# A two-layer graph network on one core: ScalarE's row-by-row tile gathers go to GpSimd, and twenty small gathers are added near the start

## The chip, the cores and the metric

The kernel runs on one core of a Trainium2 chip. The metric is device time in microseconds (us). Engines are named as the profile names them: PE is TensorE (PEld its weight loads), DVE is VectorE, ACT is ScalarE, POOL is GpSimd, SP is SyncE, which here only issues transfers. A q behind a name (ACTq, SPq) marks the work of the engine's instruction queue, such as issuing a transfer.

## The reference, cut to what matters

`x` has 12500 nodes of 256 float32 features; 200000 edges run from `src` to `dst`, sorted by `dst`.

```python
# layer 0
scale = sqrt(out_deg[src]) * sqrt(out_deg[dst])
msg   = (t1[src] + (feat[src] * feat[dst]) @ W2) / scale[:, None]     # t1 = feat @ W1
agg   = segment_sum(msg, dst)
embed = leaky_relu(where(in_cnt > 0, t1 + agg, 0) + b0)
x     = layernorm(x + embed / max(norm(embed), 1e-12))
# layer 1
xt    = x @ W.T + b1
out   = segment_sum(xt[src], dst) / (deg + 1)
x     = layernorm(x + out)
```

Both layers are linear in the gathered rows up to the sum, so the kernel gathers and sums rows of a table first (`x` scaled by the root of the degree in layer 0, the first layer's output in layer 1) and multiplies by the weights afterwards, once for each node and not for each edge.

## The kernel before

The edges are cut into tiles of 128. A **round** is 32 tiles (`U`), in four quarters or groups of 8 (`QT`, `GT`); there are 49 rounds in each of the two layers, and the last has 27 tiles. While a round's edges are summed, the two blocks of 128 nodes that the round before completed are finished (weights, activation, normalization).

**Gather.** Tile u of a round needs the 128 table rows that its edges name, 1 KB each, in slot u of `ring`, an SBUF buffer of 32 slots. For most tiles GpSimd issues one indirect transfer (`gather_quarter`, line 470): one instruction fetches all 128 rows by a column of `idx`. For tile 31 (`HAND_U`) of rounds 2 to 47 this is done otherwise, row by row. In even rounds SyncE does it (`gather_by_hand`): it loads 16 row numbers at a time into registers (line 360) and issues one transfer of one row for each (lines 362 and 363), 128 in all, into a side buffer; `hand_to_ring` (line 370) copies that into the slot once the round before is done with it. In odd rounds ScalarE does the same (`gather_by_act`, lines 631 to 635; `act_hand_to_ring`, line 641), in pieces of 24, 16 and 24 rows (`ACT_ROWS`) in each of two rounds. Both side buffers lie in space that an earlier stage has left (`src_lo`, `src_hi`). A pair of rounds has thus 62 gathers by GpSimd, 128 row transfers by SyncE and 128 by ScalarE; there are 23 pairs (`HAND_PAIRS`) in each layer.

**Sum.** VectorE builds one-hot matrices from `dst` (line 821), TensorE multiplies them with the gathered rows (line 1120), a group of 8 tiles adding up in one PSUM bank, and signals `groups_done`. VectorE adds the group to the two node blocks it can touch (line 847).

**Refill.** When a group is done, ScalarE copies the next 8 index columns for the same quarter of the next round (`refill`, line 579), which lets GpSimd gather that quarter. ScalarE's program is a fixed order: refill 0, 24 rows, refill 1, its share of finishing the last node blocks (lines 586 to 601), refill 2, two square roots that wait for VectorE (607, 609), 16 rows, refill 3, 24 rows. An instruction that waits holds up all behind it on its engine.

SyncE's order in a pair is: load and store the node blocks of one round (`next_pair`), copy its tile into the ring, wait for it, 64 rows, `next_pair` again, 64 rows, load the next 128 indices.

**Start.** GpSimd first gathers 32 tiles of raw `x` and 32 columns of the factors `r` (line 478), then waits until the scaled table is stored and a flag is made, and enters its loops. The flag chooses between this path and a slow one for unordered edges, which does not run here.

Of the kernel before, what the change touches and what calls it, by code (L numbers as in the profile page):

```python
# [24 lines left out]
P = 128  # L25
D = 256
KF = D // P
NODES = 12500
# [5 lines left out]
U = 32  # L34
# [35 lines left out]
DUMP = NPAD  # L70
HAND_U = U - 1
HAND_REGS = 16
ACT_ROWS = {0: (0, 24), 2: (24, 40), 3: (40, 64)}
HAND_PAIRS = (ROUNDS - 2) // 2


def gnn(nc, x, src, dst, w1, w2, b0, wl, b1, out):
# [6 lines left out]
    with ExitStack() as ctx:  # L84
# [19 lines left out]
        src_hi = sb("src_hi", [P, TILES], BF16)  # L104
        hands = [src_lo[:, 2 * n * D:2 * (n + 1) * D].bitcast(F32) for n in range(2)]
        hand_idxs = [src_hi[0:1, 2 * n * P:2 * (n + 1) * P].bitcast(I32) for n in range(2)]
        count_to = sb("count_to", [P, P, PAIR], BF16)
# [115 lines left out]
        gather_turn = sem("gather_turn")  # L223
        hand_idx_in = [sem(f"hand_idx_in{n}") for n in range(2)]
        hand_rows_in = [sem(f"hand_rows_in{n}") for n in range(2)]
        sync_turn = sem("sync_turn")
        hand_in_ring = [sem(f"hand_in_ring{n}") for n in range(2)]
        dst_hot_made = sem("dst_hot_made")
# [42 lines left out]
        def _(sp):  # L271
# [76 lines left out]
            def load_hand_idx(layer, j):  # L348

                sp.dma_start(hand_idxs[0][:, :],  # L350
                             src[bass.ds((2 * j + 2) * U * P + HAND_U * P, P)].rearrange("(a n) -> a n", a=1)
                             ).then_inc(hand_idx_in[0], 16)

            def gather_by_hand(layer, j, half):

                if half == 0:
                    sp.wait_ge(hand_idx_in[0], 16 * (hand_no(layer, j) + 1))
                    sp.sem_inc(sync_turn, 1)
                for first in range(half * P // 2, (half + 1) * P // 2, HAND_REGS):
                    sp.load(hand_regs, hand_idxs[0][0:1, first:first + HAND_REGS])  # L360
                    for k in range(HAND_REGS):
                        row = sp.snap(hand_regs[k], min_val=0, max_val=NODES - 1)  # L362
                        sp.dma_start(hands[0][first + k:first + k + 1, :],  # L363
                                     table[layer][bass.ds(row, 1), :]).then_inc(hand_rows_in[0], 16)

            def hand_to_ring(layer, j):

                sp.wait_ge(hand_rows_in[0], 16 * P * (hand_no(layer, j) + 1))
                sp.wait_ge(groups_done, group_no(layer, 2 * j + 1, GR - 1) + 1)
                sp.dma_start(ring[:, HAND_U, 0:D], hands[0][:, :]).then_inc(hand_in_ring[0], 16)  # L370

            def hand_pair(layer, j):

                next_pair(layer, 2 * j)
                hand_to_ring(layer, j)
                sp.wait_ge(hand_in_ring[0], 16 * (hand_no(layer, j) + 1))
# [7 lines left out]
            with sp.If(disordered == 0):  # L384
                for c in range(len(X_CHUNKS)):
                    sp.wait_ge(table_stored[c], 16)
                for layer in range(2):
# [9 lines left out]
                    hand_to_ring(layer, HAND_PAIRS - 2)  # L397
                    sp.wait_ge(hand_in_ring[0], 16 * (hand_no(layer, HAND_PAIRS - 2) + 1))
                    gather_by_hand(layer, HAND_PAIRS - 1, 0)
# [34 lines left out]
        def _(g):  # L434
# [52 lines left out]
            for u in range(RAW):  # L487
                gather_r(u)
            for c in range(len(X_CHUNKS)):
                g.wait_ge(table_stored[c], 16)  # L490
            g.wait_ge(flag_made, 1)
            disordered = g.value_load(flag[0:1, 0:1], min_val=0, max_val=1)
            with g.If(disordered == 0):
                for layer in range(2):
                    if layer == 1:
                        g.wait_ge(table1_whole, 1)
                    for i in range(0 if layer == 1 else 1, 2):
                        for q in range(4):
                            gather_quarter(layer, i, q)
                    with g.Fori(2, ROUNDS - 1) as i:  # L500
                        for q in range(4):
                            gather_quarter(layer, i, q, HAND_U)
                    for q in range(4):
                        gather_quarter(layer, ROUNDS - 1, q, FINAL)
# [25 lines left out]
        def _(act):  # L530
# [79 lines left out]

            act_regs = [act.alloc_register(f"act_row{k}") for k in range(24)]

            def act_hand_no(layer, j):

                return layer * HAND_PAIRS + j

            def load_act_idx(layer, j):

                nc.scalar.dma_start(hand_idxs[1][:, :],
                                    src[bass.ds((2 * j + 3) * U * P + HAND_U * P, P)].rearrange("(a n) -> a n", a=1)  # L620
                                    ).then_inc(hand_idx_in[1], 16)

            def gather_by_act(layer, j, half, q):

                if half == 0 and q == 0:
                    act.wait_ge(hand_idx_in[1], 16 * (act_hand_no(layer, j) + 1))
                    act.sem_inc(act_turn, 1)
                    act.wait_ge(hand_in_ring[1], 16 * (act_hand_no(layer, j) + 1))
                    act.sem_inc(act_turn, 1)
                first, end = (half * P // 2 + n for n in ACT_ROWS[q])  # L630
                act.load(act_regs[0:end - first], hand_idxs[1][0:1, first:end])  # L631
                for k in range(first, end):
                    row = act.snap(act_regs[k - first], min_val=0, max_val=NODES - 1)  # L633
                    nc.scalar.dma_start(hands[1][k:k + 1, :],  # L634
                                        table[layer][bass.ds(row, 1), :]).then_inc(hand_rows_in[1], 16)

            def act_hand_to_ring(layer, j):

                act.wait_ge(hand_rows_in[1], 16 * P * (act_hand_no(layer, j) + 1))
                act.sem_inc(act_turn, 1)  # L640
                nc.scalar.dma_start(ring[:, HAND_U, 0:D], hands[1][:, :]).then_inc(hand_in_ring[1], 16)

            def round_(layer, i, finish, pair_no=None, half=0):
                if pair_no is not None and half == 0:
                    load_act_idx(layer, pair_no)
                for q in range(4):
                    if finish and q == LAST_K + 1:
                        if layer == 0:
                            clear_sums(i - 1)
                        else:  # L650
                            act.wait_ge(groups_added, group_no(layer, i, LAST_K + 1) + SUMS)
                            take_sums(i - 1, acc[:, bass.ds(2 * i - 2, 2), :])
                        take_turned(layer, i - 1)
                    refill(layer, i, q)
                    if finish and q == LAST_K + 1:
                        roots(layer, i - 1)
                    if pair_no is not None and q in ACT_ROWS:
                        gather_by_act(layer, pair_no, half, q)
                if pair_no is not None and half == 1:
                    act_hand_to_ring(layer, pair_no)  # L660

            act.wait_ge(flag_made, 1)
            disordered = act.value_load(flag[0:1, 0:1], min_val=0, max_val=1)
            with act.If(disordered == 0):
                act.sem_inc(hand_in_ring[1], 16)
# [344 lines left out]
        def _(pe):  # L1010
# [94 lines left out]

            def round_(layer, i, finish, end=U, by_hand=None, pair_no=0):

                for k in range(GR):
# [26 lines left out]
            with pe.If(disordered == 0):  # L1135
                for layer in range(2):
                    round_(layer, 0, False)
                    round_(layer, 1, True)
                    with pe.Fori(0, HAND_PAIRS) as j:
                        round_(layer, 2 * j + 2, True, by_hand=0, pair_no=j)  # L1140
                        round_(layer, 2 * j + 3, True, by_hand=1, pair_no=j)
                    round_(layer, ROUNDS - 1, True, FINAL)
# [41 lines left out]
```

## Time and profile before

| | |
|---|---|
| timed, median of 2 runs | 4644.35 us (4642.15 to 4646.56) |
| profiled execution, from its first to its last instruction | 6311.9 us, 85381 instructions |
| PE busy | 2685.6 us (43%), 9623 matmuls |
| DVE busy | 1596.4 us (25%) |
| ACT busy | 448.2 us (7%) |
| POOL busy | 2936.4 us (47%), 3087 instructions |
| mean granted TensorE clock | 0.672 of full speed |
| DMA | 506.28 MB, 80 GB/s on average |

The profile comes from an execution of its own. The only time known of it is its span, and that is 1668 us more than the timed median: where very many small instructions are recorded, the recording takes time itself. Issuing of transfers, register work and waits are not counted as busy, so an engine can be fully occupied and still show a small share, as ScalarE and SyncE do here. The profile's chain of waits follows the work that ended last back to what released it; "issue" is time in which an engine waited for nothing that the profile shows.

### The profile page before, as it was taken

Reading aid. Unit: us, or ns where it says so; the run is one execution under the profiler, and the core shown is the slowest. Engines: PE = TensorE matmul, PEld = TensorE weight load, DVE = VectorE, ACT = ScalarE, POOL = GpSimd, SP = SyncE. Lnnn points to the kernel's source line nnn. Section 1 sums busy time; section 2 is a strip of 40 time slices with the busy share of each in tenths; the row PEclk is TensorE's granted clock in tenths of the full one; section 3 lists DMA queues with packets and bytes.
Section 4 is the critical chain, followed back from the end, with each engine's and each line's share of the span. In section 5 each row is a group of like instructions: output and inputs, shape, how many; then the busy total and the mean of one; then the engine's idle time right before and its main releaser. Section 6 shows DMA issues by size and latency. Waiting matters only on the chain.

```text
span 6311.9 us, 85381 instructions
## 1 busy us (share of the span) xinstructions
PE 2685.6 (43%) x9623; PEld 1864.3 (30%) x9623; DVE 1596.4 (25%) x3315; ACT 448.2 (7%) x1457; POOL 2936.4 (47%) x3087
## 2 busy tenths in 40 slices
PE   6344444444444444434454343434343434343434
PEld 5233333332333333323232222222232322222223
DVE  9522222222222222222231111212121212121212
ACT  9300000000000000000000000000000000000000
POOL 3444444444444444444445444444444444444444
PEclk8676666666666666666666666666666666666667
DMA  4322222222222222222222222222222222222222
GB/s 125 118 76 78 78 74 80 77 80 76 80 77 78 76 79 79 77 78 79 77 79 82 74 81 75 80 76 79 75 83 77 79 77 81 77 78 79 77 80 79
DMA packets 270181, 506.28 MB, mean 80 GB/s; under 512 B 69534, under 2 KB 172557, under 8 KB 269645
## 3 DMA queue, kind: packets, MB, share of 16 engines
q0 software_dynamic: 146656, 397.89, 22.1%
q1 hardware_dynamic: 104496, 91.77, 4.7%
q10 hardware_dynamic: 18492, 12.11, 0.7%
q14 instruction: 522, 4.27, 0.2%
q8 instruction: 15, 0.25, 0.0%
HBM read 450.89 MB, written 38.54 MB: 78 GB/s over the span
## 4 chain that ended last, share of the span: by engine, by line
SPq 45%; issue 40%; ACTq 7%; DVE 3%; PE 3%; DMA 1%; DVEq 1%; another core or an unknown queue 1%; ACT 0%
SPq L363 27%; SPq L362 9%; SPq L360 5%; ACTq L634 4%; DVE hot_space L711 2%; PE banks L1120 1%; ACTq L633 1%; ACTq L631 1%; PE banks L1099 1%; SPq L323 1%; SPq L319 1%; SPq L310 1%; DMA ring<-src_lo 1%; DVEq L703 1%
## 5 line engine op out<-in xcount | busy, mean ns | idle before, releaser
L1120 PE MATMUL banks<-ring,hot_space 128*128 128x257 f32 x6252 | 2080.3, 479 | 989.9 <-issue 931.7
L470 POOL DMA_INDIRECT ring<-x,idx x1517 | 1435.6, 946 | 1616.6 <-ACT idx L579 1130.9
L470 POOL DMA_INDIRECT ring<-scaled_x,idx x1485 | 1410.1, 950 | 1595.7 <-ACT idx L579 1161.7
L1120 PEld LDWEIGHTS banks<-ring,hot_space 128*128 128x128 f32 x6252 | 1362.8, 236 | 1657.6 <-issue 1414.6
L847 DVE SCALAR_TENSOR_TENSOR big<-banks,here_mask,big 128x257 f32 x784 | 343.1, 479 | 2835.2 <-PE banks L1120 1309.0
L1088 PE MATMUL banks<-ident,halves 128*128 128x128 f32 x588 | 140.2, 396 | 1584.3 <-ACT halves L592 1294.1
L1099 PE MATMUL banks<-w_s,a_t 128*128 128x256 f32 x784 | 285.0, 542 | 943.0 <-ACT a_t L601 943.0
L1088 PEld LDWEIGHTS banks<-ident,halves 128*128 128x128 f32 x588 | 97.2, 199 | 1630.3 <-ACT halves L592 1313.8
L821 DVE TENSOR_TENSOR hot_space<-banks,dst_rel 128x1024 f32<-128x1024 f32 x395 | 483.7, 1225 | 183.1 <-issue 182.6
L1099 PEld LDWEIGHTS banks<-w_s,a_t 128*128 128x128 f32 x784 | 218.4, 286 | 1013.3 <-ACT a_t L601 966.0
L579 ACT COPY idx<-src_col 128x8 int32 (+1 forms) x392 | 77.6, 198 | 4897.8 <-issue 4286.1
L871 DVE SCALAR_TENSOR_TENSOR e<-banks,scal,b_s 128x256 f32<-128x256 f32 x98 | 42.9, 479 | 1162.9 <-PE banks L1099 625.2
L547 ACT ACTIVATE dst_rel<-columns,halves 128x128 bf16<-128x128 f32 x576 | 161.3, 374 | 4.5 <-DVE halves L740 4.5
L857 DVE SCALAR_TENSOR_TENSOR halves<-x_t,root,big 128x256 f32<-128x256 f32 x98 | 47.4, 483 | 277.6 <-DMA x_t<-in_x 255.5
L1027 PE MATMUL banks<-hot_space 128*128 128x98 bf16 x1280 | 90.2, 235 | 41.3 <-DVE hot_space L711 40.5
L1099 PE MATMUL banks<-wt_s,a_t 128*128 128x256 f32 x392 | 107.0, 422 | 0.1
L711 DVE TENSOR_TENSOR hot_space<-src_lo,count_to 128x2048 bf16<-128x2048 bf16 x80 | 97.6, 1220 | 0.2
L1099 PEld LDWEIGHTS banks<-wt_s,a_t 128*128 128x128 f32 x392 | 89.2, 228 | 18.6 <-ACT a_t L601 0.5
L1027 PEld LDWEIGHTS banks<-hot_space 128*128 128x128 bf16 x1280 | 76.8, 113 | 52.9 <-DVE hot_space L711 45.9
L601 ACT COPY a_t<-banks 128x512 f32<-128x512 f32 (+1 forms) x196 | 87.8, 478 | 45.6 <-PE banks L1088 44.6
L478 POOL DMA_INDIRECT r_edge<-r_table,idx x32 | 31.5, 985 | 112.1 <-DMA r_table<-e 102.7
L711 DVE TENSOR_TENSOR hot_space<-src_hi,count_to 128x1568 bf16<-128x1568 bf16 x80 | 77.5, 969 | 0.0
(112 smaller groups left out, 798.8 us busy)
## 6 DMA issues: line engine op xcount, KB each, us to landing
src_lo<-scaled_x SPq DMA_DIRECT2D x2944, 1.0 KB
src_lo<-scaled_x ACTq DMA_DIRECT2D x2944, 1.0 KB
src_lo<-x SPq DMA_DIRECT2D x2944, 1.0 KB
src_lo<-x ACTq DMA_DIRECT2D x2944, 1.0 KB
ring<-x,idx POOLq DMA_INDIRECT x1517
ring<-scaled_x,idx POOLq DMA_INDIRECT x1485
x<-out_t SPq DMA_DIRECT2D x98, 128.0 KB
x_t<-x SPq DMA_DIRECT2D x98, 128.0 KB
```

The source lines that it names most:

```text
L360: sp.load(hand_regs, hand_idxs[0][0:1, first:first + HAND_REGS])
L362: row = sp.snap(hand_regs[k], min_val=0, max_val=NODES - 1)
L363: sp.dma_start(hands[0][first + k:first + k + 1, :], table[layer][bass.ds(row, 1), :]).then_inc(hand_rows_in[0], 16)
L470: g.indirect_dma_start(ring[:, u, 0:D], None, table[layer], bass.IndirectOffsetOnAxis(ap=idx[:, u:u + 1], axis=0)).then_inc(rows_in[u], 16)
L634: nc.scalar.dma_start(hands[1][k:k + 1, :], table[layer][bass.ds(row, 1), :]).then_inc(hand_rows_in[1], 16)
L711: last = nc.vector.tensor_tensor(hots[half], vals.unsqueeze(2).to_broadcast(shape), count_to[:, 0:size, :].unsqueeze(1).to_broadcast(shape ...
L821: last = nc.vector.tensor_tensor(dst_hot[:, buf, :, :], lane_row.unsqueeze(1).to_broadcast([P, GT, P]), rel, ALU.is_equal)
L847: last = nc.vector.scalar_tensor_tensor(here, group_sum(k), here_mask[:, n, bass.ds(i * GR + k, 1)], here, ALU.mult, ALU.add)
L1027: last = nc.tensor.matmul(hist, lo_hot[half][:, t // PAIR, :, t % PAIR], hi_hot[half][:, t // PAIR, :, t % PAIR], start=first and t == 0, ...
L1088: last = nc.tensor.transpose(turned[s][:, place:place + P], halves[:, s, h, k * P:(k + 1) * P], ident[:, :])
L1099: last = nc.tensor.matmul(project[s], left, right, start=n == 0, stop=n == len(parts) - 1)
L1120: last = nc.tensor.matmul(group_sum(k), dst_hot[:, k % HOTS, u - k * GT, :], ring[:, u, 0:DW], start=u == tiles[0], stop=u == tiles[-1])
```

## The change

ScalarE's gathers are removed whole: its registers, index loads, row transfers, the copy into the ring, and `ACT_ROWS`; its loop is one plain loop over rounds 1 to 48. GpSimd gathers all 32 tiles in odd rounds and 31 in even ones; its loop body holds two rounds. TensorE waits for tile 31 of an odd round on `rows_in[31]`. SyncE's part is the same with new names. New are twenty gathers from `x` by GpSimd (`LOOKS`), in five turns of four, of 128 down to 8 rows, into four slots of unused space in `src_lo` and `src_hi`; after each turn GpSimd waits until all four have landed. They stand between the gathers of `r` and the wait for the table, and nothing reads what they bring.

```diff
+LOOKS = ((P, P, P, P), (64, 64, 32, 32), (127, 127, 126, 125), (124, 120, 112, 96), (16, 16, 8, 8))
-ACT_ROWS = {0: (0, 24), 2: (24, 40), 3: (40, 64)}
...
+        looks = [part[:, 2 * n * D:2 * (n + 1) * D].bitcast(F32) for part in (src_lo, src_hi) for n in (1, 2)]
...
             for u in range(RAW):
                 gather_r(u)
+            def early_look(no, rows, slot):
+                g.indirect_dma_start(looks[slot][0:rows, :], None, x,
+                                     bass.IndirectOffsetOnAxis(ap=src_col[0:rows, no:no + 1], axis=0)
+                                     ).then_inc(looks_in[slot], 16)
+            taken = [0] * len(looks)
+            for turn, sizes in enumerate(LOOKS):
+                for slot, rows in enumerate(sizes):
+                    early_look(turn, rows, slot)
+                    taken[slot] += 16
+                for slot in range(len(sizes)):
+                    g.wait_ge(looks_in[slot], taken[slot])
+                    g.sem_inc(gather_turn, 1)
...
-                    with g.Fori(2, ROUNDS - 1) as i:
+                    with g.Fori(0, HAND_PAIRS) as j:
                         for q in range(4):
-                            gather_quarter(layer, i, q, HAND_U)
+                            gather_quarter(layer, 2 * j + 2, q, HAND_U)
+                        for q in range(4):
+                            gather_quarter(layer, 2 * j + 3, q)
...
-            def gather_by_act(layer, j, half, q):
-                if half == 0 and q == 0:
-                    act.wait_ge(hand_idx_in[1], 16 * (act_hand_no(layer, j) + 1))
-                    act.sem_inc(act_turn, 1)
-                    act.wait_ge(hand_in_ring[1], 16 * (act_hand_no(layer, j) + 1))
-                    act.sem_inc(act_turn, 1)
-                first, end = (half * P // 2 + n for n in ACT_ROWS[q])
-                act.load(act_regs[0:end - first], hand_idxs[1][0:1, first:end])
-                for k in range(first, end):
-                    row = act.snap(act_regs[k - first], min_val=0, max_val=NODES - 1)
-                    nc.scalar.dma_start(hands[1][k:k + 1, :],
-                                        table[layer][bass.ds(row, 1), :]).then_inc(hand_rows_in[1], 16)
...
                     refill(layer, i, q)
                     if finish and q == LAST_K + 1:
                         roots(layer, i - 1)
-                    if pair_no is not None and q in ACT_ROWS:
-                        gather_by_act(layer, pair_no, half, q)
-                if pair_no is not None and half == 1:
-                    act_hand_to_ring(layer, pair_no)
...
-                    with act.Fori(0, HAND_PAIRS) as j:
-                        round_(layer, 2 * j + 1, True, j, 0)
-                        round_(layer, 2 * j + 2, True, j, 1)
-                    round_(layer, ROUNDS - 2, True)
-                    round_(layer, ROUNDS - 1, True)
+                    with act.Fori(1, ROUNDS) as i:
+                        round_(layer, i, True)
...
-                        if u == HAND_U and by_hand is not None:
-                            pe.wait_ge(hand_in_ring[by_hand], 16 * (layer * HAND_PAIRS + pair_no + 1 + by_hand))
+                        if u == HAND_U and by_hand:
+                            pe.wait_ge(hand_in_ring, 16 * (layer * HAND_PAIRS + pair_no + 1))
                         elif u == HAND_U:
-                            pe.wait_ge(rows_in[u], 16 * (layer * 2 + i + 1))
+                            rounds_before = layer * (HAND_PAIRS + 2) + (i if pair_no is None else pair_no + 2)
+                            pe.wait_ge(rows_in[u], 16 * (rounds_before + 1))
```

## Rows read from the trace of the kernel before

**Rows 1.** The page: span, and the chain that ended last by engine.
```profile
span 6311.9 us, 85381 instructions
...
SPq 45%; issue 40%; ACTq 7%; DVE 3%; PE 3%; DMA 1%; DVEq 1%; another core or an unknown queue 1%; ACT 0%
```

**Rows 2.** Line 470, GpSimd's gathers: ns min/median/max; then idle us, times, until whom.
```profile
L470 POOL DMA_INDIRECT ring<-x,idx x1517: 940/946/1207, 3277.1 to 6284.9; - x190
L470 POOL DMA_INDIRECT ring<-scaled_x,idx x1485: 940/946/1195, 254.3 to 3232.7; - x186
...
  ACT idx L579: 2292.5, 288
```

**Rows 3.** Timeline of GpSimd: start us, us, instruction, [idle before, us, <- its releaser].
```profile
227.00 0.94 POOL L478 DMA_INDIRECT r_edge<-r_table,idx  x1 [0.30 <-issue]
254.33 0.94 POOL L470 DMA_INDIRECT ring<-scaled_x,idx  x1 [26.39 <-ACT idx L579]
...
297.97 0.95 POOL L470 DMA_INDIRECT ring<-scaled_x,idx  x1 [0.30 <-issue]
...
3200.23 0.94 POOL L470 DMA_INDIRECT ring<-scaled_x,idx  x1 [9.61 <-ACT idx L579]
...
3277.11 0.94 POOL L470 DMA_INDIRECT ring<-x,idx  x1 [43.44 <-SPq L337]
...
3369.54 0.94 POOL L470 DMA_INDIRECT ring<-x,idx  x1 [4.16 <-ACT idx L579]
...
6247.58 0.94 POOL L470 DMA_INDIRECT ring<-x,idx  x1 [9.08 <-ACT idx L579]
```

**Rows 4.** Waits over the whole span: who, for what: us, times, longest.
```profile
ACT idx L579 <- issue: 4286.1, 273, 24.3
```

**Rows 5.** Timeline of ScalarE in one steady pair of rounds, 1505 to 1649 us.
```profile
1508.18 13.01 ACTq L634 DMA_DIRECT2D src_lo<-scaled_x  x24
1521.46 0.20 ACT L579 COPY idx<-src_col 128x8 int32 x1 [14.94 <-issue]
...
1535.67 13.02 ACTq L634 DMA_DIRECT2D src_lo<-scaled_x  x16
...
1550.82 15.08 ACTq L634 DMA_DIRECT2D src_lo<-scaled_x  x24
...
1574.12 13.12 ACTq L634 DMA_DIRECT2D src_lo<-scaled_x  x24
...
1602.01 12.79 ACTq L634 DMA_DIRECT2D src_lo<-scaled_x  x16
...
1616.92 14.46 ACTq L634 DMA_DIRECT2D src_lo<-scaled_x  x24
...
1633.54 14.11 ACTq L634 DMA_DIRECT2D src_lo<-scaled_x  x24
```

**Rows 6.** Timeline of SyncE's row transfers in four stretches.
```profile
231.96 22.03 SPq L363 DMA_DIRECT2D src_lo<-scaled_x  x46
...
256.27 37.96 SPq L363 DMA_DIRECT2D src_lo<-scaled_x  x24
...
1502.65 58.08 SPq L363 DMA_DIRECT2D src_lo<-scaled_x  x64
...
1564.65 50.97 SPq L363 DMA_DIRECT2D src_lo<-scaled_x  x64
...
1628.88 9.86 SPq L363 DMA_DIRECT2D src_lo<-scaled_x  x18
...
3280.11 65.11 SPq L363 DMA_DIRECT2D src_lo<-x  x24
```

**Rows 7.** Timeline of ScalarE, 3143 to 3154 us, in which SyncE issues nothing.
```profile
3143.10 10.49 ACTq L634 DMA_DIRECT2D src_lo<-scaled_x  x24
```

**Rows 8.** Timeline of TensorE at the start of the second layer.
```profile
3280.01 9.78 PE L1120 MATMUL banks<-ring,hot_space 128*128 128x257 f32 x16 [12.59 <-DMA ring<-x,idx]
...
3312.25 1.20 PE L1120 MATMUL banks<-ring,hot_space 128*128 128x257 f32 x2 [3.00 <-issue]
```

More of the change, by code:

```diff
@@ L104, in gnn @@
         src_hi = sb("src_hi", [P, TILES], BF16)
-        hands = [src_lo[:, 2 * n * D:2 * (n + 1) * D].bitcast(F32) for n in range(2)]
-        hand_idxs = [src_hi[0:1, 2 * n * P:2 * (n + 1) * P].bitcast(I32) for n in range(2)]
+        hand = src_lo[:, 0:2 * D].bitcast(F32)
+        hand_idx = src_hi[0:1, 0:2 * P].bitcast(I32)
+        looks = [part[:, 2 * n * D:2 * (n + 1) * D].bitcast(F32) for part in (src_lo, src_hi) for n in (1, 2)]
         count_to = sb("count_to", [P, P, PAIR], BF16)
@@ L223, in gnn @@
         gather_turn = sem("gather_turn")
-        hand_idx_in = [sem(f"hand_idx_in{n}") for n in range(2)]
-        hand_rows_in = [sem(f"hand_rows_in{n}") for n in range(2)]
+        looks_in = [sem(f"looks_in{n}") for n in range(len(looks))]
+        hand_idx_in = sem("hand_idx_in")
+        hand_rows_in = sem("hand_rows_in")
         sync_turn = sem("sync_turn")
-        hand_in_ring = [sem(f"hand_in_ring{n}") for n in range(2)]
+        hand_in_ring = sem("hand_in_ring")
         dst_hot_made = sem("dst_hot_made")
@@ L348, in load_hand_idx @@
             def load_hand_idx(layer, j):
-                sp.dma_start(hand_idxs[0][:, :],
+                sp.dma_start(hand_idx[:, :],
                              src[bass.ds((2 * j + 2) * U * P + HAND_U * P, P)].rearrange("(a n) -> a n", a=1)
-                             ).then_inc(hand_idx_in[0], 16)
+                             ).then_inc(hand_idx_in, 16)
             def gather_by_hand(layer, j, half):
                 if half == 0:
-                    sp.wait_ge(hand_idx_in[0], 16 * (hand_no(layer, j) + 1))
+                    sp.wait_ge(hand_idx_in, 16 * (hand_no(layer, j) + 1))
                     sp.sem_inc(sync_turn, 1)
                 for first in range(half * P // 2, (half + 1) * P // 2, HAND_REGS):
-                    sp.load(hand_regs, hand_idxs[0][0:1, first:first + HAND_REGS])
+                    sp.load(hand_regs, hand_idx[0:1, first:first + HAND_REGS])
                     for k in range(HAND_REGS):
                         row = sp.snap(hand_regs[k], min_val=0, max_val=NODES - 1)
-                        sp.dma_start(hands[0][first + k:first + k + 1, :],
-                                     table[layer][bass.ds(row, 1), :]).then_inc(hand_rows_in[0], 16)
+                        sp.dma_start(hand[first + k:first + k + 1, :],
+                                     table[layer][bass.ds(row, 1), :]).then_inc(hand_rows_in, 16)
             def hand_to_ring(layer, j):
-                sp.wait_ge(hand_rows_in[0], 16 * P * (hand_no(layer, j) + 1))
+                sp.wait_ge(hand_rows_in, 16 * P * (hand_no(layer, j) + 1))
                 sp.wait_ge(groups_done, group_no(layer, 2 * j + 1, GR - 1) + 1)
-                sp.dma_start(ring[:, HAND_U, 0:D], hands[0][:, :]).then_inc(hand_in_ring[0], 16)
+                sp.dma_start(ring[:, HAND_U, 0:D], hand[:, :]).then_inc(hand_in_ring, 16)
             def hand_pair(layer, j):
@@ L375, in hand_pair @@
                 hand_to_ring(layer, j)
-                sp.wait_ge(hand_in_ring[0], 16 * (hand_no(layer, j) + 1))
+                sp.wait_ge(hand_in_ring, 16 * (hand_no(layer, j) + 1))
                 gather_by_hand(layer, j + 1, 0)
@@ L397, in _ @@
                     hand_to_ring(layer, HAND_PAIRS - 2)
-                    sp.wait_ge(hand_in_ring[0], 16 * (hand_no(layer, HAND_PAIRS - 2) + 1))
+                    sp.wait_ge(hand_in_ring, 16 * (hand_no(layer, HAND_PAIRS - 2) + 1))
                     gather_by_hand(layer, HAND_PAIRS - 1, 0)
@@ L609, in roots, with round_ @@
                 nc.scalar.activation(pair[3], mv[:, :, 1], ACT.Sqrt, bias=epsilon[:, 0:1]).then_inc(var_rooted, 1)
[L611 to L621, printed above, removed]
-            def gather_by_act(layer, j, half, q):
-                if half == 0 and q == 0:
-                    act.wait_ge(hand_idx_in[1], 16 * (act_hand_no(layer, j) + 1))
-                    act.sem_inc(act_turn, 1)
-                    act.wait_ge(hand_in_ring[1], 16 * (act_hand_no(layer, j) + 1))
-                    act.sem_inc(act_turn, 1)
-                first, end = (half * P // 2 + n for n in ACT_ROWS[q])
-                act.load(act_regs[0:end - first], hand_idxs[1][0:1, first:end])
-                for k in range(first, end):
-                    row = act.snap(act_regs[k - first], min_val=0, max_val=NODES - 1)
-                    nc.scalar.dma_start(hands[1][k:k + 1, :],
-                                        table[layer][bass.ds(row, 1), :]).then_inc(hand_rows_in[1], 16)
[L637 to L645, printed above, removed]
+            def round_(layer, i, finish):
                 for q in range(4):
@@ L664, in _ @@
             with act.If(disordered == 0):
-                act.sem_inc(hand_in_ring[1], 16)
                 for c in range(len(X_CHUNKS)):
@@ L1104, in pace, with round_ @@
                 pe.value_load(block_row[0:1, 0:1], min_val=0, max_val=NW - 1)
-            def round_(layer, i, finish, end=U, by_hand=None, pair_no=0):
+            def round_(layer, i, finish, end=U, by_hand=False, pair_no=None):
                 for k in range(GR):
@@ L1139, in _ @@
                     with pe.Fori(0, HAND_PAIRS) as j:
-                        round_(layer, 2 * j + 2, True, by_hand=0, pair_no=j)
-                        round_(layer, 2 * j + 3, True, by_hand=1, pair_no=j)
+                        round_(layer, 2 * j + 2, True, by_hand=True, pair_no=j)
+                        round_(layer, 2 * j + 3, True, pair_no=j)
                     round_(layer, ROUNDS - 1, True, FINAL)
```

## The prediction

> **What bounds the kernel now.** I read the head of the page and the chain first, then the waits of GpSimd and ScalarE, then both engines' instructions in one stretch. All durations come from the one profiled execution, whose span is 6311.9 us; the timed runs have a median of 4644.35 us, 1668 us less [rows 1]. So the recording itself stretches this kernel, most where single instructions are many, and SyncE's share of the chain (45%) is to be read with that in mind. I make the sum against 6311.9 us and then scale only the repeated rounds to the timed median.
>
> GpSimd needs 1.25 us from one gather to the next, whether its queue has just started or has run for many gathers [rows 2, 3]. In the recording it stands still before a gather for 2292.5 us because ScalarE has not yet refilled the indices [rows 2], and ScalarE's refill waits mostly for nothing but its own queue (4286.1 us put down to "issue") [rows 4]. The stretch shows why: after each refill ScalarE issues 24, 16 or 24 row transfers, and the next refill stands right behind the last of them [rows 5]. So in the recording ScalarE sets the pace: refill, rows, refill.
>
> Is this so in the timed runs? The steady rounds 2 to 47 run from 297.97 to 3200.23 us in the first layer and from 3369.54 to 6247.58 us in the second [rows 3]: 5780.3 us for 46 pairs of rounds, 125.7 us each. All the rest is 531.6 us. If that rest costs the same when timed, a timed pair is (4644.4 - 531.6) / 46 = 89.4 us. What can fill 89.4 us? **GpSimd:** 62 gathers x 1.25 = 77.5 us. **SyncE:** 46 rows alone took 22.03 us with their register loads, 0.479 us each [rows 6]; 128 rows are 61.3 us, and between its blocks of 64 rows it spends 3.9 and 13.3 us on loads, stores and the copy into the ring (1560.73 to 1564.65, 1615.62 to 1628.88) [rows 6]: 78.5 us. **ScalarE:** 24 rows alone took 10.49 us, 0.437 each [rows 7], so 128 are 55.9 us; of the pair from 1508.18 to 1633.54 us its six row blocks fill 81.5 us and everything else 43.9 us [rows 5]: 99.8 us. ScalarE is the only one of the three that reaches 89.4 us; part of its 43.9 us (waits for VectorE) must be shorter when timed. I take it as the bound.
>
> **The change part by part.** (1) ScalarE loses, in each of 46 pairs, 128 row transfers with their register work, six register loads, an index load and the copy into the ring. Its queue falls from 99.8 us to at most 43.9 us a pair, below the others, and each refill stands behind the matmuls of its own quarter again. Gain: what the next bound allows. (2) GpSimd gets 46 gathers, 46 x 1.25 = 57.5 us; it will be the bound, so I count them in full: 63 x 1.25 = 78.75 us a pair. The loop body doubles to two rounds, which costs nothing between instructions that follow each other at 0.30 us of issue [rows 3]. (3) TensorE waits for tile 31 of an odd round on that gather's own semaphore instead of the copy into the ring. The gather is GpSimd's last of the round, as late as the copy was or earlier; behind this wait stand the group's end, the VectorE sum and the refill, all of which have three quarters of gathers (some 30 us) as slack: nothing. (4) SyncE keeps its 128 rows a pair, 78.5 us by the floor above. It no longer shares issue time with ScalarE: with ScalarE busy its 64 rows took 58.08 and 50.97 us, 0.91 and 0.80 a row, against 0.479 alone [rows 6].
>
> (5) The twenty early gathers. GpSimd's last gather of r starts at 227.00 us and is over at 228.2 us, and the first table gather waits until 254.33 us [rows 3], for an index refill that hangs on TensorE's first group and not on GpSimd. Twenty gathers at 1.25 us are 25 us. At each of five turns GpSimd waits for the data: from a gather's start at 3277.11 us to the matmul that uses it at 3280.01 us are 2.9 us [rows 3, 8], 1.65 us beyond the pitch, 8.3 us in all. So GpSimd comes to the first table gather at 261.5 us, 7 us late. The trace shows no gather of fewer rows: between a floor of the 0.30 us gap alone (then the idle time hides all, 0 us) and data landing as slowly as beside SyncE's rows (4.2 us from tile to tile [rows 8], 13 us more) the bounds are 0 and 20 us; I take 7, since nearest is the full gather. Behind these waits stand only GpSimd's own gathers.
>
> **The sum.** A pair after: GpSimd 78.75 us, SyncE 78.5 us. Two bounds this close never overlap fully, and gathers slow SyncE's rows: in two stretches with gathers running and ScalarE silent it issued 24 rows in 37.96 and 65.11 us, 1.58 and 2.71 a row [rows 6]. That cannot hold when timed: 128 rows fit into 89.4 - 17.2 = 72.2 us now, 0.564 a row at most. I take 81 us a pair. In the profiled frame: 6311.9 - 5780.3 + 7 = 538.6 us, plus 46 x 81 = 3726: 4265 us. For the likeliest case pairs of 78.75 to 84 us give 4161 and 4403; with 0 for the early gathers 4154. Own range 4150 to 4400.
>
> The row says that issuing a transfer takes ScalarE 0.437 us and that this is what the refills wait for. The Trainium skill (DMA: Bandwidth & Descriptors, "Issuing engines are not separate DMA queues") says that spreading transfers over engines only saves issue time, "usually small relative to the DMA itself"; by it ScalarE's rows would cost next to nothing and their removal would bring nothing, which is the first rival's time.
>
> **The rivals.** *A, GpSimd is already the bound when timed.* Then its gather takes 89.4 / 62 = 1.442 us there, though 1.25 us in the trace, and the change adds 46 x 1.442 = 66 us and some 8 us for the early gathers: 4718 us. For it: the recording's shape is ScalarE's and need not be that of the timed runs. Against it: gathers never slow down with load in the trace (at most 1.207 us busy against a median of 0.946 [rows 2]), and recording adds time, it does not take any away. The Trainium skill (SBUF — State Buffer, "Who interferes with whom") says that GpSimd's generation of descriptors can be shut out while VectorE holds the shared port; that would speak for this rival, and the trace does not agree: 1.207 us is the longest of 3002.
>
> *B, SyncE is the next bound.* The sum holds until its average row passes (78.75 - 17.2) / 128 = 0.481 us. Halfway to today's 0.564, at 0.53, a pair is 85 us: 538.6 + 3910 = 4449 us. For it: 78.5 against 78.75 leaves no room.
>
> *C, slower.* The same queue, starved. Gathers run 77.5 of 89.4 us now and nearly without a break afterwards, and beside them rows are slow [rows 6]. The hand-gathered tile then comes late each second round. It decides from a row of 0.579 us, where a pair reaches 91.3 us and the whole 4737 us; at 0.60 us a pair is 94.0 us and the whole 4863 us. For it: the two slow stretches. Against it: 256 rows and 62 gathers fit into 89.4 us today, the change leaves 128 rows and 63 gathers.
>
> **How the numbers follow.** Forecast 0.55; A 0.20; B 0.15; C 0.10. Predicted 4265 us. The range runs from 4150 (all hidden, GpSimd alone) up to 4720, which takes in B and A's value and leaves out C and the edges. 2% is 93 us (below 4551, above 4737), about what can be told from no change. Faster: forecast and B, 0.70. Same: nearly all of A, and half of what B and C put near the border, 0.20. Slower: C and A's edge, 0.10.
>
> **What would show it.** In the profile after, GpSimd's waits for the refill should fall from 2292.5 us to a few hundred, ScalarE's refill should wait for TensorE's group instead of "issue", GpSimd's pitch should stay 1.25 us, and the first table gather should start near 261 us. SyncE's rows should be nearer 0.48 than 0.9 us where no gathers run. The recorded span should fall less surely than the timed one, because recording stretches SyncE's rows. It would be wrong if GpSimd stood idle as long as before with tile 31 of even rounds late (B, C), or if the timed pair grew by one gather (A).

## The result, and the profile after

The changed kernel takes 4153.61 us (2 runs, 4153.19 to 4154.04) against 4644.35 us: a ratio of 0.893, 95% interval 0.8885 to 0.8979. The forecast was faster and about 4265 us; the gain is 491 us and not 379. Multiplied out, 0.8932 of the median before is 4148 us, just under the low end of the range.

One thing must be said first, since it decides how the recording before is to be read. **The recording of before was made in other surroundings than its timed runs.** A recording does not stretch this kernel: after, the span is 4152.3 us beside timed runs of 4153.6. The kernel before, timed again in five later batches (a batch is a set of kernels timed side by side), took 4640, 6302, 6376, 4641 and 6412 us, and within a batch its runs agreed within 1%. I call these the quick and the slow surroundings. The recording of before (6311.9 us, [rows 1]) was made in the slow surroundings, the 4644.35 us were timed in the quick. What differs between them outside the kernel isn't known: two of the batches, one quick (4640 us) and one slow (6376 us), were reported under the same chip number.

The head and the chain of the page after, and two waits from the trace (who, for what: us, times, longest):

```profile
span 4152.3 us, 67120 instructions
...
POOL 70%; issue 25%; ACT 2%; DMA 1%; PE 1%; POOLq 1%; DVE 1%; DVEq 0%; ACTq 0%; SPq 0%
...
ACT idx L598 <- PE banks L1098: 2511.2, 388, 34.4
...
POOL ring L472 <- issue: 931.6, 3046, 3.5
```

The chain is GpSimd's gathers (line 472 now) with the gap of 0.30 us between them: 70% and 25%. ScalarE's refill (line 598 now) waits for TensorE's group and no longer for its own queue (4286.1 us in [rows 4]). Line 472 by itself, after:

```profile
L472 POOL DMA_INDIRECT ring<-x,idx x1540: 942/946/1215, 2200.1 to 4133.3; - x193
L472 POOL DMA_INDIRECT ring<-scaled_x,idx x1508: 942/946/1226, 275.1 to 2168.8; - x189
its engine sat idle before it (us, times) until:
  issue: 931.6, 3046
  SPq L339: 30.3, 1
  ACT idx L598: 0.3, 1
```

A gather costs what it cost in [rows 2] (median 946 ns), and the wait for the refill has gone to 0.3 us. The 2292.5 us of [rows 2] are from the slow surroundings; the first experiment below, recorded in the quick ones with ScalarE's rows in place, has 641.9 us, and that is the number to compare with:

```profile
POOL ring L473 <- ACT idx L597: 641.9, 224, 9.0
```

GpSimd's timeline after, answering to [rows 3]:

```profile
275.07 0.98 POOL L472 DMA_INDIRECT ring<-scaled_x,idx  x1 [3.48 <-issue]
...
315.33 1.03 POOL L472 DMA_INDIRECT ring<-scaled_x,idx  x1 [0.30 <-issue]
...
2135.95 0.99 POOL L472 DMA_INDIRECT ring<-scaled_x,idx  x1 [0.30 <-issue]
...
2280.06 0.95 POOL L472 DMA_INDIRECT ring<-x,idx  x1 [0.31 <-issue]
...
4100.75 0.95 POOL L472 DMA_INDIRECT ring<-x,idx  x1 [0.30 <-issue]
```

From the second row to the third and from the fourth to the fifth are 23 pairs of rounds each: 1820.6 and 1820.7 us, 79.16 us a pair, of which 63 gathers are 78.75. All the rest is 511.0 us. SyncE's row transfers after:

```profile
1513.51 31.29 SPq L365 DMA_DIRECT2D src_lo<-scaled_x  x64
...
1549.82 31.19 SPq L365 DMA_DIRECT2D src_lo<-scaled_x  x64
```

64 rows in 31.3 us, 0.489 each, beside gathers without a break; the recording of the first experiment, with ScalarE's rows in place, has the same 31.3 us. In [rows 6] rows beside gathers took up to 2.71 us; that was the slow surroundings.

### The profile page after: what moved, and what is told of

It reads as the page before. It is cut to its first block, busy times and chain, and to the rows that moved or that the text cites. A ratio compares the mean times of both kernels' runs of the same rounds, so it can differ in the third digit from the quotient of the medians.

```text
span 4152.3 us, 67120 instructions
## 1 busy us (share of the span) xinstructions
PE 3222.2 (78%) x9623; PEld 1713.0 (41%) x9623; DVE 1603.0 (39%) x3315; ACT 460.6 (11%) x1457; POOL 3015.1 (73%) x3153
## 3 DMA queue, kind: packets, MB, share of 16 engines
q1 hardware_dynamic: 104496, 91.77, 7.0%
## 4 chain that ended last, share of the span: by engine, by line
POOL 70%; issue 25%; ACT 2%; DMA 1%; PE 1%; POOLq 1%; DVE 1%; DVEq 0%; ACTq 0%; SPq 0%
POOL ring L472 68%; ACT dst_rel L566 2%; POOL r_edge L480 1%; DMA src_hi<-in_x,src_col 0%; POOL src_lo L494 0%; PE banks L1076 0%; POOLq L469 0%; DVEq L680 0%; DMA ring<-x,idx 0%; POOLq L470 0%; PE banks L1098 0%; POOLq L517 0%; ACTq L566 0%; DMA ring<-scaled_x,idx 0%; PE banks L1065 0%
## 5 line engine op out<-in xcount | busy, mean ns | idle before, releaser
L1098 PE MATMUL banks<-ring,hot_space 128*128 128x257 f32 x6252 | 2745.4, 551 | 817.3 <-DMA ring<-x,idx 374.5
L1098 PEld LDWEIGHTS banks<-ring,hot_space 128*128 128x128 f32 x6252 | 1281.3, 247 | 2214.3 <-DMA ring<-x,idx 1020.0
L472 POOL DMA_INDIRECT ring<-x,idx x1540 | 1464.9, 951 | 499.5 <-issue 468.9
L472 POOL DMA_INDIRECT ring<-scaled_x,idx x1508 | 1435.5, 952 | 462.7 <-issue 462.7
L1076 PE MATMUL banks<-w_s,a_t 128*128 128x256 f32 x784 | 185.1, 390 | 0.0
L1076 PEld LDWEIGHTS banks<-w_s,a_t 128*128 128x128 f32 x784 | 147.6, 193 | 34.5 <-issue 15.7
L1065 PEld LDWEIGHTS banks<-ident,halves 128*128 128x128 f32 x588 | 115.2, 209 | 45.8 <-issue 21.3
L1076 PEld LDWEIGHTS banks<-wt_s,a_t 128*128 128x128 f32 x392 | 72.2, 194 | 26.6 <-issue 17.9
L903 DVE TENSOR_SCALAR out_t<-out_t,mv,scal 128x256 f32<-128x256 f32 x196 | 75.4, 426 | 7.7
## 6 DMA issues: line engine op xcount, KB each, us to landing
x<-out_t SPq DMA_DIRECT2D x98, 128.0 KB
x_t<-x SPq DMA_DIRECT2D x98, 128.0 KB
x_t<-in_x SPq DMA_DIRECT2D x97, 128.0 KB
```

The source lines that it names most:

```text
L472: g.indirect_dma_start(ring[:, u, 0:D], None, table[layer], bass.IndirectOffsetOnAxis(ap=idx[:, u:u + 1], axis=0)).then_inc(rows_in[u], 16)
L903: nc.vector.tensor_scalar(out_t[s][:, :], out_t[s][:, :], mv[:, s, 0:1], scal[:, 6 + s:7 + s], ALU.subtract, ALU.mult).then_inc(out_ready[ ...
L1065: last = nc.tensor.transpose(turned[s][:, place:place + P], halves[:, s, h, k * P:(k + 1) * P], ident[:, :])
L1076: last = nc.tensor.matmul(project[s], left, right, start=n == 0, stop=n == len(parts) - 1)
L1098: last = nc.tensor.matmul(group_sum(k), dst_hot[:, k % HOTS, u - k * GT, :], ring[:, u, 0:DW], start=u == tiles[0], stop=u == tiles[-1])
```

## The experiments

Two theories stood at first. Q: ScalarE's queue is too long for a pair of rounds, and the early gathers only cost their time. G: the early gathers change how gathers and row transfers share the DMA path, which would explain SyncE's sudden 0.489 us. Times are medians of 4 runs against 7 of the kernel before in the same batch, but for the last experiment.

**Early gathers on the kernel before.** The `LOOKS` block of the change is put into the kernel before, ScalarE's rows stay.

> The kernel before with the twenty early gathers added and ScalarE's row transfers kept. Theory Q (ScalarE's queue is the bound, the early gathers only cost their time at the start): 4644 + 21 = about 4665 us, SyncE's rows beside gathers as slow as before (1.6 to 2.7 us each). Theory G (the early gathers change how later gathers and row transfers share the DMA engines; the profile after has SyncE's rows at 0.50 us beside unbroken gathers): clearly under 4644 us, some 4250 to 4500 us, and SyncE's rows near 0.5 to 0.7 us.

4686.2 us beside 4640.1, ratio 1.0098 (1.0077 to 1.0119): 46 us more, where Q had said 21. G, which wanted a clear gain, is out. This is also a quick recording of ScalarE's part (line 652 issues its rows, 597 is the refill; timeline of one pair of rounds):

```profile
1522.56 9.43 ACTq L652 DMA_DIRECT2D src_lo<-scaled_x  x24
1532.27 0.20 ACT L597 COPY idx<-src_col 128x8 int32 x1 [12.19 <-issue]
...
1545.83 6.23 ACTq L652 DMA_DIRECT2D src_lo<-scaled_x  x16
...
1554.16 9.43 ACTq L652 DMA_DIRECT2D src_lo<-scaled_x  x24
...
1565.74 9.14 ACTq L652 DMA_DIRECT2D src_lo<-scaled_x  x24
...
1589.43 6.12 ACTq L652 DMA_DIRECT2D src_lo<-scaled_x  x16
...
1597.67 9.45 ACTq L652 DMA_DIRECT2D src_lo<-scaled_x  x24
```

The six blocks of rows take 49.8 us, 0.39 us a row, of a pair of 90.7 us. The other 40.9 us are not all work: 20.8 us of them, in this pair, ScalarE waits for VectorE before the square roots. The chain of this recording is ScalarE's queue:

```profile
ACTq 47%; issue 20%; PE 11%; DVE 6%; ACT 5%; DMA 4%; DVEq 4%; POOL 3%; SPq 0%; POOLq 0%
```

**No early gathers; all of 128 rows; a single one of 127.**

```diff
-LOOKS = ((P, P, P, P), (64, 64, 32, 32), (127, 127, 126, 125), (124, 120, 112, 96), (16, 16, 8, 8))
+LOOKS = ()                     # e2, and e15 again
+LOOKS = ((P, P, P, P),) * 5    # e3
+LOOKS = ((127,),)              # e4
```

> The changed kernel without any of the twenty early gathers. Theory Q: 4153.6 less the 21 us by which the first table gather starts later, about 4133 us. Theory G: SyncE's rows are slow again wherever gathers run, tile 31 of the even rounds comes late, and most of the gain is gone: 4450 us or more.

> The changed kernel with twenty early gathers that are all of 128 rows. Theory Q: about 4150 us. Theory G in the form that it is the uneven row counts (127, 126, 125, 124, 120, 8) that shift something: as the kernel without early gathers, 4450 us or more if that one is slow. Theory G in the form that any gather at that place does it: 4150 us.

> The changed kernel with a single early gather, of 127 rows. Theory Q: about 4133 us. Theory G in the form of uneven row counts: one such gather already shifts it, about 4133 us with fast rows, or a time in between if the size of the shift matters.

4118.8 us without any (ratio 0.8873, 0.8857 to 0.8889), 4149.2 us with twenty of 128 rows (0.8937) and 4119.5 us with a single one (0.8872). The early gathers cost some 30 to 35 us here and bring nothing; one alone costs nothing that shows. In a later batch the kernel without any took 4115.3 us beside 4640.8, ratio 0.8864 (0.8849 to 0.8879):

> The changed kernel without early gathers. Beside a before of 4640 us: 4119 us again. Beside a before of 6300 us or more: if the early gathers have no part in the slow regime, about 35 us under the changed kernel's 7009 us, some 6970 us; if they made it slow, near or below the kernel before.

**Fewer rows by ScalarE**, from the kernel before. The rows left out are stale in the sum, and the wait before the copy into the ring counts 96 or 64 rows.

```diff
-ACT_ROWS = {0: (0, 24), 2: (24, 40), 3: (40, 64)}
+ACT_ROWS = {0: (0, 16), 2: (16, 32), 3: (32, 48)}   # 96 rows: e6, e10, e14
+ACT_ROWS = {0: (0, 8), 2: (8, 16), 3: (16, 32)}     # 64 rows: e7, e11, e16
```

> The kernel before with ScalarE fetching 96 rows of its tile (pieces of 16, 16 and 16 in each round) in place of 128; 32 rows of that tile are left stale. Theory Q (the time that ScalarE's queue needs for a pair of rounds is the bound): ScalarE saves 32 x 0.392 = 12.5 us of the 90.6 us of a pair, 78.1 us are left beside GpSimd's 77.5, so 473 + 46 x 78.1 = about 4066 us. Rival D (row transfers cost through the DMA engines they share with the gathers, each row the same): a quarter of the gain, about 4490 us.

> The kernel before with ScalarE fetching 64 rows of its tile (8, 8 and 16 in each round); 64 rows are left stale. Theory Q: ScalarE's queue needs 65.5 us a pair, GpSimd's 62 gathers 77.9 us, so it is flat from the kernel with 96 rows on: about 4056 us. Rival D: half of the gain, about 4350 us.

> The kernel with ScalarE fetching 96 of 128 rows once more, because the kernel before needed 6302 us in that run's company and not 4640 us: the surroundings, not the kernel, had changed (theory S: there are two regimes of the DMA path, and the recording of before was made in the slow one). If the kernel before takes about 4640 us this time, theory Q gives about 4066 us and rival D about 4490 us, as stated for the first run. If it takes about 6300 us, theory S says that this one takes about 6230 us again.

> As before with 64 rows. Beside a before of 4640 us: theory Q about 4056 us, rival D about 4350 us. Beside a before of 6300 us: about 6430 us again.

> ScalarE with 96 rows, for the normal surroundings. Beside a before of 4640 us: theory Q (length of ScalarE's queue) about 4066 us, rival D (each row costs through the shared DMA path) about 4490 us. Beside a before of 6300 to 6376 us: 0.989 of it, as twice before.

> ScalarE with 64 rows, for the normal surroundings. Beside a before of 4640 us: theory Q says flat, since GpSimd's 62 gathers are the bound from 96 rows on: 4056 to 4110 us. Rival D: 4640 us less half of its gain, and clearly less than the 96-row kernel's 4110 us. Beside 6300 us or more: 1.02 of before.

Only e14 fell into quick surroundings: 4110.2 us beside 4640.8, ratio 0.8857 (0.8836 to 0.8878). A quarter fewer rows, with the tile, its copy and all other rows in place, gives the whole gain (4115.3 us in the same batch with no row by ScalarE), and GpSimd's wait for the refill falls from 641.9 to 74.1 us; of the two times in its expectation, 4066 (Q) and 4490 us (D), the first is the near one. Its blocks of 16 rows take 6.1 to 6.4 us:

```profile
1539.01 6.14 ACTq L634 DMA_DIRECT2D src_lo<-scaled_x  x16
...
1546.80 6.40 ACTq L634 DMA_DIRECT2D src_lo<-scaled_x  x16
```

In the slow surroundings 96 rows gave ratios of 0.989 and 0.989, and 64 rows 1.019, 1.021 and 1.017: there ScalarE's rows are not the bound, and 53 to 55% of the chain of these five recordings is SyncE's queue. So whether 64 rows are flat against 96 in quick surroundings was not measured.

**Every tile by GpSimd**, from e2: SyncE's rows are gone as well, and TensorE waits for each tile on its gather.

```diff
                         for q in range(4):
-                            gather_quarter(layer, 2 * j + 2, q, HAND_U)
+                            gather_quarter(layer, 2 * j + 2, q)
...
-                    with sp.Fori(0, HAND_PAIRS - 2) as j:
-                        hand_pair(layer, j)
+                    with sp.Fori(0, 2 * HAND_PAIRS - 1) as m:
+                        next_pair(layer, m)
```

> The changed kernel without early gathers, and with SyncE's row transfers gone too: GpSimd gathers every tile. If GpSimd's queue alone is the bound there, a pair is 64 gathers, 80.4 us, and the whole 473 + 46 x 80.4 = 4171 us, 52 us over the 4119 us with SyncE's tile. If SyncE's rows slow the gathers or TensorE at all, less than that, down to 4119 us or below.

> Every tile gathered by GpSimd. Beside a before of 4640 us: 4171 us (GpSimd's queue, 80.4 us a pair). Beside a before of 6300 us: about 5047 us again, by theory S because gathers land late there even with no row transfer in the kernel.

> Every tile by GpSimd. Beside a before of 4640 us: 4171 us, 46 x 1.25 us over the kernel without early gathers (4115 to 4119 us). Beside 6300 us or more: 0.79 to 0.80 of before, as twice.

5046.6, 5056.3 and 5054.8 us, all in slow surroundings, ratios 0.799, 0.794 and 0.788. So there SyncE's and ScalarE's rows together cost a fifth of the time, and what stays above the 4171 us expected in quick surroundings comes with no row transfer at all. GpSimd and TensorE in the second of these runs:

```profile
1511.99 0.94 POOL L460 DMA_INDIRECT ring<-scaled_x,idx  x1 [3.41 <-issue]
...
1536.15 1.20 PE L1081 MATMUL banks<-ring,hot_space 128*128 128x257 f32 x2 [9.86 <-issue]
1539.67 1.22 PE L1081 MATMUL banks<-ring,hot_space 128*128 128x257 f32 x2 [2.32 <-issue]
1543.85 1.20 PE L1081 MATMUL banks<-ring,hot_space 128*128 128x257 f32 x2 [2.96 <-issue]
1545.97 8.91 PE L1081 MATMUL banks<-ring,hot_space 128*128 128x257 f32 x26 [0.92 <-issue]
```

The first row is the gather of the tile that TensorE starts in the second, 24 us later, and GpSimd had issued gathers without a break in between. TensorE waits 9.9 us before that tile and soon after takes 13 tiles (26 records) in 8.9 us: the gathers are seen late. That is the pattern of [rows 8]. Whether they landed late or TensorE's own queue was slow to see them, the trace does not say.

**The refill by VectorE**, from the kernel before: the copy of line 579 moves into VectorE's program behind its sum of the group.

```diff
-                nc.scalar.copy(idx[:, q * QT:(q + 1) * QT], src_col[:, bass.ds(i * U + U + q * QT, QT)]).then_inc(idx_ready, 1)
...
                 last.then_inc(groups_added, 1)
+                nc.vector.tensor_copy(idx[:, k * QT:(k + 1) * QT], src_col[:, bass.ds(i * U + U + k * QT, QT)]).then_inc(idx_ready, 1)
```

> The kernel before, ScalarE's rows and waits kept, but the index refill of each group done by VectorE behind its sum of that group. Theory Q1 (it is the total of ScalarE's queue that is too long: its part in finishing the node blocks comes once a round whatever else moves): 4640 us within 1%. Theory Q2 (only the refill's place behind the rows hurts): GpSimd no longer waits, near 4060 us.

> The kernel before with the index refill done by VectorE. Beside a before of 4640 us: theory Q1 (the total of ScalarE's queue) 4640 us within 1%; theory Q2 (the refill's place behind the rows) near 4060 us. Beside 6300 us or more: 1.14 of before.

7180.8 and 7253.1 us, ratios 1.139 and 1.133, both in slow surroundings, where neither theory had a number at first. Whether the total of ScalarE's queue or the refill's place in it counted in quick ones is not settled.

**The changed kernel in slow surroundings.**

> The changed kernel itself. Beside a before of 4640 us: 4154 us. Beside a before of 6300 us, theory S: it is slowed as well, to 5300 to 6200 us, since SyncE's 128 rows a pair run beside gathers; the theory that the early gathers keep the slow regime away: 4154 us.

7009.2 us against 6376.1: ratio 1.101 (1.098 to 1.103). **The change is a loss of 10% there.** I had expected a time below before. SyncE's timeline and GpSimd's wait in this recording:

```profile
1525.89 63.73 SPq L365 DMA_DIRECT2D src_lo<-scaled_x  x64
...
1593.54 62.86 SPq L365 DMA_DIRECT2D src_lo<-scaled_x  x64
...
POOL ring L472 <- ACT idx L598: 2854.5, 166, 35.2
PE banks L1098 <- DMA ring<-src_lo: 889.6, 23, 39.8
```

The same 64 rows take 63 us in place of 31, a pair 140.0 us, and 126.6 of it are SyncE's rows. GpSimd stands idle, TensorE waits for SyncE's tile (the last line).

What is slow there is not only the transfers. The register operations on SyncE's queue that prepare a row and move nothing (ns min/median/max), in the slow recording of before and in the quick one of after:

```profile
L362 SPq FUSED_REGOPS  x5888: 2/44/1400, 231.8 to 6201.8; - x197
...
L364 SPq FUSED_REGOPS  x5888: 44/44/56, 231.6 to 4019.7; - x197
```

The packets of SyncE's queue took the same time in both: 4.7% of 16 engines' 6311.9 us and 7.0% of their 4152.3 us, over 104496 packets, are some 45 ns each. So the slow surroundings hold up SyncE's queue as it issues, and not the moving of its bytes. And they do so beside gathers. Counted over whole traces, mean time from one row to the next within a block of 64, by whether GpSimd had begun a gather in the 3 us before:

| | no gather near | a gather near |
|---|---|---|
| before, slow | 0.49 us | 1.22 us |
| the changed kernel, slow (e13) | 0.48 us | 2.09 us |
| the changed kernel, quick | 0.50 us | 0.49 us |

Of the 5888 register operations in the slow recording of before, 676 of the 2957 near a gather took over 0.3 us, and 16 of the other 2931. Why gathers hold up another engine's queue in some batches and not in others is not known.

**The kernel before, recorded again.**

> The kernel before unchanged, for a recording in normal surroundings. Theory S: its recorded span equals its time, about 4640 us, ScalarE's rows take 0.39 us each and stand between the refills, and a pair takes 90.6 us. If it is the recording itself that stretches this kernel: a span near 6300 us beside timed runs of 4640 us.

A single run; it fell beside a before of 6412 us: time 6423.5 us, span 6421.7 us. The recording adds nothing, the surroundings do. A pair takes 128.0 us, SyncE's rows of it 118.3:

```profile
1519.89 58.85 SPq L363 DMA_DIRECT2D src_lo<-scaled_x  x64
1583.02 59.42 SPq L363 DMA_DIRECT2D src_lo<-scaled_x  x64
```

## Why the prediction was right or wrong, step by step

**The bound (right for the timed runs, in part by luck).** In quick surroundings ScalarE's queue set the pair. Estimated were 99.8 us for it against a timed pair of 89.4; a quick recording shows 49.8 us of rows and 40.9 us of all else in 90.7 us (forecast 55.9 and 43.9). Shown by e14: a quarter of the rows less and the time is 4110 us. But the sentence "in the recording ScalarE sets the pace" was wrong of the recording that it was read from: in such surroundings a quarter of the rows less gave 1.1%, and without ScalarE's rows the kernel lost 10%. There the chain's 45% for SyncE [rows 1] was the better guide, and the prediction had put it aside as an effect of recording.

**"So the recording itself stretches this kernel" (wrong).** It does not. This was the step that failed, and others hang on it. The rest outside the 46 pairs was taken over as 531.6 us from a slow recording; in quick surroundings it is 473.0 us (e2). With the early gathers, 538.6 us were forecast and 511.0 measured: 28 us of the miss. Two errors partly cancel in it: the rest was 59 us too high, the early gathers 31 us too low (7 for 38).

**The pair after (size off, the largest part of the miss).** I took 81 us because two bounds so close would not overlap fully and gathers would slow SyncE's rows. Neither happened: the pair is 79.16 us, GpSimd's own 78.75 and 0.4, and GpSimd waits for nobody. The 46 pairs make 85 us of the miss; with the 28 us above that is the whole distance from 4265 to the span of 4152. The slow rows of [rows 6] belong to the slow surroundings.

**46 gathers more for GpSimd at 1.25 us (right).** The pitch holds with and without load; e2 at 4119 us and a pair of 79.16 us show it as the bound.

**The early gathers (mis-sized).** Forecast 7 us with bounds of 0 and 20. The first table gather starts at 275.07 us, against 238.09 us in e2: 37 us, and 30 to 35 us in the total (46 us on the kernel before). Two errors: GpSimd's idle time to cover them was 26.4 us in [rows 3] but is 9.2 us in e2; and the twenty take 46.3 us, not 33.3. Twenty full gathers take 40.4 us (e3), so 7 us of that are mostly waits taken too short and 6 us come of the smaller sizes: "nearest is the full gather" did not hold, as in the recording after those of 127 rows took 2.54 us.

```profile
244.74 2.54 POOL L494 DMA_INDIRECT src_lo<-in_x,src_col  x1 [2.44 <-DMA src_hi<-in_x,src_col]
247.59 2.54 POOL L494 DMA_INDIRECT src_lo<-in_x,src_col  x1 [0.31 <-issue]
...
259.76 1.29 POOL L494 DMA_INDIRECT src_lo<-in_x,src_col  x1 [6.85 <-DMA src_hi<-in_x,src_col]
```

The first two are the gathers of 127 rows. The third, of 124 rows and of the next turn, waited 6.85 us, by the profile for a gather into `src_hi`, which are those of 126 and 125 rows: the four of that turn took 7.1 to 10.4 us to land, four of 128 rows in the first turn 2.7 to 3.6.

**Rivals.** A (GpSimd already the bound) is out: its wait for the refill was real, 641.9 us in e1, and its pitch in a quick recording is 1.25 us and not 1.442. One argument against it was too broad, though: "gathers never slow down with load" holds for the 3002 table gathers, but in the same recording the 32 gathers of raw `x` at the start took 1.7 us each:

```profile
L474 POOL DMA_INDIRECT ring<-in_x,idx x32 | 54.6, 1708 | 23.7 <-DVE halves L740 14.3 <-issue 9.4
```

They run beside VectorE's counting of the edges (line 711, two inputs from SBUF). In e2's recording the one at 41.90 us, begun while VectorE stood still for 0.43 us, took 0.94 us and the one before it 1.72. That VectorE is the cause was not tested, but "the trace does not agree", as the prediction has it, was too strong. In the repeated rounds, which set the time, the median is 946 ns before and after.

B (SyncE next) is out in quick surroundings: its rows take 0.489 us, a little over the 0.481 I had put as the limit, but its gaps, with all waits in them, are 16.7 us a pair and not 17.2, and GpSimd never waits. It has next to nothing to spare. C (SyncE starved, slower) did not happen in the runs forecast; its time is what comes in the slow surroundings: 17.2 + 128 x 0.99 = 144 us by its formula, 140.0 measured. Its mechanism fits too, with one difference: what is held up beside gathers is SyncE's whole queue, register operations too, and not its transfers alone. My argument against it, that 256 rows and 62 gathers fit into 89.4 us, joined a time from the quick surroundings to a trace from the slow; inside that trace alone 128 rows of SyncE nearly filled the pair already.

**Marks named in advance.** GpSimd's waits for the refill "a few hundred": 0.3 us. Refill waiting for TensorE: yes. Pitch 1.25 us: yes. First table gather near 261 us: 275. SyncE's rows near 0.48: 0.489. "The recorded span should fall less surely than the timed one": no, it is the time.

## What to carry to other kernels

When the recorded span and the timed median differ by a third, ask first whether both come from the same surroundings, before blaming the recording; sums may only be made inside one of them. A kernel whose engines issue single-row transfers beside a stream of gathers can gain 11% in one place and lose 10% in the other from the same edit, so time it beside the old one in several batches. An in-order queue that both refills another engine's work and issues many small transfers is a bound that no busy share shows: add up its issue time for one period and compare that with the period. Keep its waits apart in that sum: with them in it, every in-order queue fills the period.

## What the runs showed of the hardware that was not expected

The kernel before took 4640 us or 6300 to 6412 us by batch, with nothing changed; in the recordings of slow batches SyncE's 64 rows beside gathers took 59 to 64 us and not 31, and register operations on its queue up to 1.4 us and not 56 ns at most; both only where gathers ran, but for a few. A gather of 127 rows took GpSimd 2.54 us against 0.95 for one of 128; alone (e4) it held up the first table gather until 241.28 us, 3.2 us later than with none:

```profile
229.00 2.55 POOL L494 DMA_INDIRECT src_lo<-in_x,src_col  x1 [0.30 <-issue]
241.28 0.96 POOL L472 DMA_INDIRECT ring<-scaled_x,idx  x1 [9.73 <-issue]
```

The gathers of 126 and of 125 rows, in this order, stand right behind those of 127 in the changed kernel's turn:

```profile
250.43 0.98 POOL L494 DMA_INDIRECT src_hi<-in_x,src_col  x1 [0.30 <-issue]
251.71 1.21 POOL L494 DMA_INDIRECT src_hi<-in_x,src_col  x1 [0.30 <-issue]
```

The Trainium skill (DMA: Bandwidth & Descriptors, section "Why a DMA increments its semaphore by 16 and not by 1") says that a DMA uses the largest number of engines, up to 16, that divides its number of rows. Worked out from that rule, and so an estimate, 127 rows get one engine, 126 get fourteen, 125 get five, and 128 get sixteen. The trace agrees in order: 2.54, 0.98, 1.21 and 0.95 us, and the first three were the same in the recording of e1. For 124 rows (four engines) it has 1.29 and 1.55 us. Which engines served them the trace does not name, and the rows are not all that counts: a gather of 128 rows in the first turn took 1.86 us, begun 0.2 us after an instruction of VectorE (line 805, two inputs from SBUF).

That a queue of single rows can be a bound was expected, but it is worth its numbers: the same page (section "Issuing engines are not separate DMA queues") says that the time to issue a DMA is usually small relative to the DMA itself. That compares a single DMA with its own issue, and how long a single row needs to land the trace does not say; SyncE's queue takes 0.489 us to issue a row, and its packets took some 45 ns each. What counts in this kernel is the sum over an in-order queue: in the recording of e1 six blocks of single rows held ScalarE's queue for 49.8 of 90.7 us. There the measurement decides.
